# The shared expert's down product split into three short-format products, in an attention and mixture-of-experts block

## The chip, the cores and the metric

The kernel runs on one core of a Trainium2 chip, as one program. The metric is its device time in microseconds, the median of several executions. A profile is taken from one more execution.

## The reference

x has 8 batches of 256 tokens with 256 features. First a modulated layer norm and attention with 16 query and 8 key heads; its result goes through a gate and is added to x. Then the part that matters here: a second modulated norm, an RMS norm, and two things added up: 32 routed experts (each token goes to four of them, with at most 128 tokens per expert), and one shared expert that every token passes:

```python
sh = jax.nn.silu(x @ sw_gate) * (x @ sw_up) @ sw_down   # 256 -> 704 -> 256
sh = jax.nn.sigmoid(x @ w_shared_gate) * sh
out = out + sh
return inp + out.reshape(Bq, Sq, Hq)
```

All arrays are float32.

## The kernel before

The 2048 tokens are handled as four pairs of batches, q = 0 to 3, 512 tokens each. The text calls them quarters. The order of work of each engine is written out by hand, one function per engine, and semaphores join the engines. Each engine runs its instructions in the written order.

**Attention** takes the first 566 us: 128 steps, with the work after attention for pair q spread over the steps of pair q+1 (`hooks`). The last pair has no such cover, and its work (`post_gate`, `post_stats`, `post_h2`, `post_squares`, `post_rms`, `post_xn`, `post_xnt`, then logits, choice of experts, slots) is mixed by hand with the shared expert of pair 0.

**The shared expert** of a quarter has two parts. `gate_up(q, f)` makes inner rows in six pieces, f = 0 to 5: five of 128 rows and one of 64 (704 = 5 x 128 + 64). Each piece is made with 12 products of 512 columns (6 in the last piece, where gate and up share one), in the short format: sums of hi x hi, hi x lo and lo x hi, where hi is the value rounded to the format float32r and lo is what is left (`halves`, lines 1287 to 1293). ScalarE then takes the silu of the gate (`silu_of`, into one of two halves of `sg2`), and VectorE multiplies it by the up part (`hidden`, into `hs`). `down(q, t)` (lines 1482 to 1494) makes the 128 output rows of token tile t, t = 0 to 3, by six float32 products, one for each piece, of 128 tokens by 256 features. The result is scaled and put into `shrow`.

**Order after attention.** Gate/up of quarter 0 (two pieces already between the last attention steps), down of quarter 0 around the last pair's router (`post_logits`, `post_prefix`), gate/up and down of quarter 1, the 32 experts (`expert_slot`), then gate/up and down of quarters 2 and 3. While quarters 2 and 3 run, GpSimd and VectorE combine the experts' sums (`combine`): GpSimd for quarters 1 and 2, VectorE for quarters 0 and 3, VectorE's steps for quarter 3 lying between its `hidden(LAST, ...)`.

**Queues.** Loads go out from SP in a fixed order. The experts' weights and rows sit in a ring of eight, and a load for expert e waits until expert e - 8 has been used. The first rows of experts are loaded when all scatters are done (`st_scat`); GpSimd issues these, and some of them wait for a tile or a piece of quarter 1 (`PRODUCT`, `TILE`, lines 816 to 823).

**Memory.** Buffers are laid out like a stack; what is allocated after `att.close()` lies where attention's buffers were.

Of the kernel before, what the change touches and what calls it, by code (L numbers as in the profile page):

```python
# [5 lines left out]
F32 = mybir.dt.float32  # L6
# [44 lines left out]
def adaln_block(nc, x, w_pack, w_o, conv_k, conv_v, w_norm, w_router, w_gate, w_up, w_down, sw_gate, sw_up,  # L51
                sw_down, w_sgate, c_in, wmod, cos_t, sin_t, mask_t, ident_t, tri_t, ebase_t, out):
    ctx = ExitStack()
    with ctx:
# [127 lines left out]
        hs = sb("hs", [PN, FT, TOK])  # L182
        sg2 = sb("sg2", [PN, 2, TOK])
        swd = sb("swd", [PN, FT, H])
        shrow = sb("shrow", [PN, NPAIR * TT, H])
# [8 lines left out]
        gball = sb("gball", [PN, B, H])  # L194
        fin = sb("fin", [PN, NPAIR, TT, H])
        first_sums = sb("first_sums", [PN, NSUM, TT, H])
# [25 lines left out]
        def gu_banks(q, f):  # L222
# [43 lines left out]
            sem(n) for n in ("sw_hi_done", "sw_lo_done", "sh_ps", "sg2_done", "hs_done", "dn_ps", "shrow_done"))  # L266

# [203 lines left out]
        def _(act):  # L471
# [184 lines left out]
            def silu_of(q, f):  # L656
                act.wait_ge(sh_ps, FT * q + (f + 1))
                if f >= 2 or later(q):
                    act.wait_ge(hs_done, FT * q + (f - 1))
                gate, up = gu_banks(q, f)  # L660
                if f < FT - 1:
                    act.activation(sg2[:, f % 2, :], gate[:, :], ACT.Silu).then_inc(sg2_done, 1)
                else:
                    act.activation(sg2[0:FR, f % 2, :], up[FR:2 * FR, :], ACT.Silu).then_inc(sg2_done, 1)

            def shared_rows(q, t):
                act.wait_ge(dn_ps, TT * q + (t + 1))
                act.activation(shrow[:, TT * q + t, :], DN[t % 2][:, 0:H], ACT.Copy, scale=sgate[:, q, t:t + 1]).then_inc(shrow_done, 1)
# [15 lines left out]
            silu_of(0, 1)  # L684
            silu_of(0, 2)
            act.preload_act_table_set("natural_log_exp_and_others")
            post_std(LAST, 0, 2)
            silu_of(0, 3)
            post_squares(LAST, 0)
# [3 lines left out]
            silu_of(0, 4)  # L693
            silu_of(0, 5)
            post_xnt(LAST, 0)
# [5 lines left out]
            for f in range(FT):  # L701
                silu_of(1, f)
# [4 lines left out]
            for q in range(2, NPAIR):  # L707
                for f in range(FT):
                    silu_of(q, f)
# [6 lines left out]
        def _(pool):  # L716
# [123 lines left out]
            def with_shared(q):  # L840

                rows_q = shrow[:, TT * q:TT * (q + 1), :]
# [14 lines left out]
            def combine(q):  # L857
                a = sums(q, 0)
                pool.wait_ge(ld_sums[q], 16 * NSUM)
                for i in range(1, NSUM):  # L860
                    own(pool.tensor_tensor(a, a, sums(q, i), ALU.add))
                own(pool.tensor_tensor(batches(a), batches(a), gate_of(q), ALU.mult))
                f = fin[:, q, :, :]
                if q == 1:
                    pool.tensor_tensor(f, f, a, ALU.add).then_inc(fin_done[q], 1)
                else:
                    pool.wait_ge(ld_bas[q], 16)
                    own(pool.tensor_tensor(f, f, a, ALU.add))
                    pool.wait_ge(shrow_done, TT * (q + 1))
                    pool.tensor_tensor(f, f, shrow[:, TT * q:TT * (q + 1), :], ALU.add).then_inc(fin_done[q], 1)  # L870
# [6 lines left out]
        def _(dve):  # L877
# [293 lines left out]
            def hidden(q, f):  # L1171
# [30 lines left out]
            for f in range(FT):  # L1202
                hidden(1, f)
# [53 lines left out]
            def shared_rows(q, t):  # L1257
                dve.wait_ge(dn_ps, TT * q + (t + 1))
                dve.scalar_tensor_tensor(shrow[:, TT * q + t, :], DN[t % 2][:, 0:H], sgate[:, q, t:t + 1],
# [5 lines left out]
            for f in range(FT):  # L1265
                hidden(2, f)
# [7 lines left out]
            hidden(LAST, 1)  # L1274
            combine(LAST, 3)
            for f in range(2, FT):
                hidden(LAST, f)
            for t in range(TT):
                shared_rows(LAST, t)
                dve.wait_ge(shrow_done, TT * LAST + (t + 1))  # L1280
                dve.tensor_tensor(fin[:, LAST, t, :], fin[:, LAST, t, :], shrow[:, TT * LAST + t, :],
# [4 lines left out]
        def _(pe):  # L1286
# [289 lines left out]
            pe.wait_ge(ld_swd, 32)  # L1576
# [67 lines left out]
```

## Time and profile before

| | us |
|---|---|
| median of 3 runs | 781.05 (780.67 to 781.09) |
| the profiled execution, device time | 779.91 |
| its span, first to last instruction | 778.1 |
| TensorE busy | 744.3 (96% of the span) |
| weight loads busy | 617.3 (79%) |
| VectorE, ScalarE, GpSimd busy | 536.7, 441.9, 425.7 |
| granted TensorE clock, mean | 0.998 |

In the profile PE is TensorE's products, PEld its weight loads, DVE VectorE, ACT ScalarE, POOL GpSimd, and SP the engine whose queue carries most of the DMAs. A row of the chain of waits says from when, for how long and by whom the path to the end was held. A busy TensorE is not TensorE at its peak: records of products overlap, so their pace is read from starts and from pieces of the chain, not from the length of a single record. An f32 product appears as two records, a short-format product as one.

### The profile page before, as it was taken

To read this page: it belongs to the slowest core of one execution; us is meant where nothing else is said; L and a number is where in the kernel's file an instruction comes from. 1 tells how busy PE (TensorE), PEld (TensorE's weight loads), DVE (VectorE), ACT (ScalarE), POOL (GpSimd) and SP (SyncE) were. 2 spreads that over 40 slices of the span, in tenths; PEclk is the share of its full clock that TensorE was granted. 3 is DMA by queue.
4 is the path that set the end of the run, shared out by engine and by line. 5 is a ranking of instruction groups with operands and counts; after the bars stand their busy time and mean duration, and the time that the engine had idled before them with its cause. 6 is when DMAs were issued, how large, how long until landed. Compare 5 with 4: busy or idle time off the path is not lost.

```text
span 778.1 us, 12285 instructions
## 1 busy us (share of the span) xinstructions
PE 744.3 (96%) x3858; PEld 617.3 (79%) x3858; DVE 536.7 (69%) x1676; ACT 441.9 (57%) x1145; POOL 425.7 (55%) x337
## 2 busy tenths in 40 slices
PE   3899999999999999999999999999989999989998
PEld 3688778888888888788888888888876777756765
DVE  4698777679877777987786798778664234534283
ACT  4687766766876576677657667766553222212110
POOL 0644445554556378646637865654544527656366
PEclk9999999999999999999999999999999999999999
DMA  8950006700005011100401101050358669997762
GB/s 301 313 130 1 2 1 207 249 1 1 1 1 174 17 39 47 39 0 1 141 23 39 46 28 45 31 161 2 122 148 265 147 189 288 271 253 149 183 203 81
DMA packets 62351, 84.45 MB, mean 109 GB/s; under 512 B 6312, under 2 KB 50229, under 8 KB 62288
## 3 DMA queue, kind: packets, MB, share of 16 engines
q1 hardware_dynamic: 52880, 73.52, 31.1%
q0 software_dynamic: 7680, 8.95, 5.8%
q10 hardware_dynamic: 1728, 1.21, 0.6%
q8 instruction: 31, 0.51, 0.3%
q14 instruction: 32, 0.26, 0.1%
HBM read 54.88 MB, written 33.51 MB: 114 GB/s over the span
## 4 chain that ended last, share of the span: by engine, by line
PE 78%; DVE 10%; DMA 5%; ACT 3%; issue 2%; SPq 1%; POOL 1%; ACTq 0%; POOLq 0%
PE PJ L1292 23%; PE OUT L1396 12%; PE U L1385 6%; PE U L1345 6%; PE U L1374 5%; DMA xe<-slot_rows 4%; PE U L1546 3%; PE U L1344 3%; PE U L1386 3%; PE OUT L1492 3%; PE U L1492 3%; PE U L1292 2%; PE XB L1292 2%; PE XB L1368 1%; DVE U L945 1%
## 5 line engine op out<-in xcount | busy, mean ns | idle before, releaser
L736 POOL TENSOR_TENSOR qsw<-qsw,sinT 128x512 f32<-128x512 f32 x96 | 124.2, 1294 | 214.8 <-ACT qsw L523 214.1
L536 ACT ACTIVATE U<-U,nmax 128x128 f32<-128x128 f32 (+1 forms) x256 | 98.9, 386 | 79.2 <-DVE nmax L945 79.0
L945 DVE CUSTOM_DVE_ANT_0 U<-U,mask 128x128 f32<-128x128 f32 (+1 forms) x256 | 86.6, 379 | 74.9 <-PE U L1345 74.7
L1396 PE MATMUL OUT<-wo,oT 128*128 128x256 f32 x512 | 131.5, 380 | 0.0
L1292 PE MATMUL PJ<-hT_hi,w_hi 128*128 128x512 f32 x256 | 113.5, 443 | 4.3 <-DVE hT_lo L919 3.9
L1292 PE MATMUL PJ<-hT_lo,w_hi 128*128 128x512 f32 x256 | 102.2, 399 | 0.0
L1292 PE MATMUL PJ<-hT_hi,w_lo 128*128 128x512 f32 x256 | 102.2, 399 | 0.0
L955 DVE TENSOR_SCALAR prob<-U,rinv 128x128 f32<-128x128 f32 (+1 forms) x256 | 95.1, 413 | 4.5
L522 ACT ACTIVATE qsw<-PJ 64x512 f32<-64x512 f32 x96 | 57.0, 593 | 67.1 <-PE PJ L1292 61.7
L740 POOL TENSOR_TENSOR qr<-qr,qsw 128x512 f32<-128x512 f32 x64 | 82.9, 1295 | 18.5 <-DVE qr L933 14.8
L1396 PEld LDWEIGHTS OUT<-wo,oT 128*128 128x128 f32 x512 | 87.6, 191 | 6.6
L747 POOL DMA_INDIRECT slot_rows<-xn,sidx x64 | 64.4, 1006 | 44.2 <-issue 11.1
L1385 PE MATMUL U<-pT,vN 128*128 128x256 f32 x256 | 77.0, 382 | 1.9 <-ACT pT L544 1.8
L1345 PE MATMUL U<-kc,qr 128*128 128x256 f32 x256 | 76.8, 382 | 0.0
L830 POOL DMA_INDIRECT expert_sum<-ye,slot_token x32 | 49.7, 1552 | 42.3 <-DMA expert_sum<-ye,slot_token 22.4
L544 ACT ACTIVATE pT<-U 128x384 f32<-128x384 f32 x128 | 62.4, 488 | 9.4 <-PE U L1374 5.7
L1374 PE MATMUL U<-ident,prob 128*128 128x128 f32 x384 | 62.9, 273 | 0.4 <-DVE prob L955 0.4
L1344 PEld LDWEIGHTS U<-kc,qr 128*128 128x128 f32 x256 | 47.7, 190 | 19.1 <-issue 4.6
L1374 PEld LDWEIGHTS U<-ident,prob 128*128 128x128 f32 x384 | 49.9, 141 | 13.5 <-DVE prob L955 0.8
L1292 PEld LDWEIGHTS PJ<-hT_hi,w_hi 128*128 128x128 f32 x256 | 49.1, 192 | 13.0 <-DVE hT_lo L919 4.3
L1292 PEld LDWEIGHTS PJ<-hT_hi,w_lo 128*128 128x128 f32 x256 | 49.1, 192 | 11.7
L960 DVE COPY oT<-U 128x256 f32<-128x256 f32 x128 | 54.0, 422 | 4.9 <-PE U L1386 4.9
(201 smaller groups left out, 1557.3 us busy)
## 6 DMA issues: line engine op xcount, KB each, us to landing
wgu<-in_dram SPq DMA_DIRECT2D x32, 352.0 KB
expert_sum<-blank SPq DMA_DIRECT2D x3, 2176.0 KB, 17.7
wd<-in_dram SPq DMA_DIRECT2D x16, 352.0 KB
slot_rows<-blank SPq DMA_DIRECT2D x1, 4624.0 KB, 26.8
xe<-slot_rows SPq DMA_DIRECT2D x16, 289.0 KB
late_sums<-expert_sum SPq DMA_DIRECT2D x9, 512.0 KB, 9.8
wraw<-in_dram SPq DMA_DIRECT2D x8, 512.0 KB, 12.1
bcm<-mod_rows SPq DMA_DIRECT2D x8, 512.0 KB, 6.7
```

What stands on the lines that cost most here:

```text
L536: last = act.activation(U[n % 3][:, a:z], U[n % 3][:, a:z], ACT.Exp, scale=-1.0, bias=nmax[:, n % 4, j:j + 1], accum_out=rsum[:, n % 4, j: ...
L736: pool.tensor_tensor(pair3(qsw[:, n % NQSW, :]), pair3(qsw[:, n % NQSW, :]), both(sinT[:, :]), ALU.mult).then_inc(t2_done, 1)
L740: pool.tensor_tensor(rope_buffer(m), rope_buffer(m), qsw[:, n % NQSW, :], ALU.add).then_inc(rope_done, 1)
L747: pool.indirect_dma_start(out=slots_d, out_offset=bass.IndirectOffsetOnAxis(ap=sidx[:, c:c + 1], axis=0), in_=xn[:, p % 2, c // TOPK, :], ...
L945: last = dve.tensor_tensor_reduce(out=U[n % 3][:, a:z], in0=U[n % 3][:, a:z], in1=mask[:, a:z], scale=-float(HD) ** -0.5, scalar=3.4e38, o ...
L955: last = dve.tensor_scalar(prob[:, n % 2, a:z], U[n % 3][:, a:z], rinv[:, n % 4, j:j + 1], None, ALU.mult)
L1292: last = pe.matmul(out_ap, a(c), b_(c), start=(n == 0), stop=(n == len(steps) - 1))
L1344: pe.matmul(U[n % 3][:, 0:PN], q[:, 0:PN], k[:, 0:PN], start=True, stop=True)
L1345: pe.matmul(U[n % 3][:, PN:3 * PN], q[:, PN:S], k, start=True, stop=True).then_inc(sc_ps, 1)
L1374: last = pe.transpose(U[n % 3][:, j * PN:(j + 1) * PN], prob[:, n % 2, j * PN:(j + 1) * PN], ident[:, :])
L1385: pe.matmul(o, v[:, 0:PN], pT[:, n % 2, 0:S], start=True, stop=False)
L1396: last = pe.matmul(OUT[b][:, t * H:(t + 1) * H], oT[:, n % NOT, t * PN:(t + 1) * PN], wo[:, head, :], start=(head == 0 and t == 0), stop=( ...
```

## The change

The down product gets the same form as gate/up. Both of its operands are split. ScalarE makes the high parts by a copy into float32r (`hidden_high` for a piece of the inner rows, `down_high` once for the weights), and VectorE makes the low parts by subtraction (`hidden_low`, `down_low`). `hidden` now writes its product in place into `sg2`, and so a half of `sg2` is free for the next silu only when `hidden_low` has read it: `silu_of` waits for `hs_lo_done` of the piece two before. `down` waits for `hs_lo_done` where it waited for `hs_done`, and has 18 products in place of six. `gate_up` still waits for `hs_done`. `shrow` keeps two quarters instead of four, `sums` of quarter 0 lie over the experts' buffers, and `gball` and `fin` move down.

```diff
-        hs = sb("hs", [PN, FT, TOK])
+        hs_hi = sb("hs_hi", [PN, FT, TOK], F32R)
+        hs_lo = sb("hs_lo", [PN, FT, TOK], F32R)
         sg2 = sb("sg2", [PN, 2, TOK])
-        swd = sb("swd", [PN, FT, H])
-        shrow = sb("shrow", [PN, NPAIR * TT, H])
+        raw_d = ExitStack()
+        swd = sb("swd", [PN, FT, H], F32, raw_d)
+        raw_d.close()
+        shrow = sb("shrow", [PN, 2 * TT, H])
+        swd_hi = sb("swd_hi", [PN, FT, H], F32R)
+        swd_lo = sb("swd_lo", [PN, FT, H], F32R)
+        gball = sb("gball", [PN, B, H])
+        fin = sb("fin", [PN, NPAIR, TT, H])
+
+        sums_at = ExitStack()
+        first_sums = sb("first_sums", [PN, NSUM, TT, H], F32, sums_at)
+        sums_at.close()
...
@@ ScalarE
                 if f >= 2 or later(q):
-                    act.wait_ge(hs_done, FT * q + (f - 1))
+                    act.wait_ge(hs_lo_done, FT * q + (f - 1))
...
+            def hidden_high(q, f):
+                fw = min(PN, FS - f * PN)
+                act.wait_ge(hs_done, FT * q + (f + 1))
+                if f == 0 and later(q):
+                    act.wait_ge(dn_ps, TT * q)
+                act.activation(hs_hi[0:fw, f, :], sg2[0:fw, f % 2, :], ACT.Copy).then_inc(hs_hi_done, 1)
+
+            def down_high():
+                act.wait_ge(ld_swd, 32)
+                act.activation(swd_hi[:, 0:FT - 1, :], swd[:, 0:FT - 1, :], ACT.Copy)
+                act.activation(swd_hi[0:FR, FT - 1, :], swd[0:FR, FT - 1, :], ACT.Copy).then_inc(swd_hi_done, 1)
...
             silu_of(0, 0)
             silu_of(0, 1)
+            hidden_high(0, 0)
             silu_of(0, 2)
+            hidden_high(0, 1)
             act.preload_act_table_set("natural_log_exp_and_others")
             post_std(LAST, 0, 2)
             silu_of(0, 3)
+            hidden_high(0, 2)
+            down_high()
             post_squares(LAST, 0)
             post_squares(LAST, 1)
             act.preload_act_table_set("natural_log_exp_and_others")
             post_rms(LAST)
             silu_of(0, 4)
+            hidden_high(0, 3)
             silu_of(0, 5)
+            hidden_high(0, 4)
+            hidden_high(0, 5)
             post_xnt(LAST, 0)
             post_xnt(LAST, 1)
             shared_rows(0, 0)
...
-            for f in range(FT):
-                silu_of(1, f)
+            for f in range(FT + 1):
+                if f < FT:
+                    silu_of(1, f)
+                if f > 0:
+                    hidden_high(1, f - 1)
...
@@ VectorE
                 dve.wait_ge(sg2_done, FT * q + (f + 1))
-                if f == 0 and later(q):
-                    dve.wait_ge(dn_ps, TT * q)
-                dve.tensor_tensor(hs[0:fw, f, :], gu_banks(q, f)[1][0:fw, :], sg2[0:fw, f % 2, :], ALU.mult).then_inc(hs_done, 1)
+                g = sg2[0:fw, f % 2, :]
+                dve.tensor_tensor(g, gu_banks(q, f)[1][0:fw, :], g, ALU.mult).then_inc(hs_done, 1)
+
+            def hidden_low(q, f):
+                fw = min(PN, FS - f * PN)
+                dve.wait_ge(hs_hi_done, FT * q + (f + 1))
+                dve.tensor_tensor(hs_lo[0:fw, f, :], sg2[0:fw, f % 2, :], hs_hi[0:fw, f, :].bitcast(F32),
+                                  ALU.subtract).then_inc(hs_lo_done, 1)
+
+            def down_low():
+                dve.wait_ge(swd_hi_done, 1)
+                dve.tensor_tensor(swd_lo[:, 0:FT - 1, :], swd[:, 0:FT - 1, :], swd_hi[:, 0:FT - 1, :].bitcast(F32), ALU.subtract)
+                dve.tensor_tensor(swd_lo[0:FR, FT - 1, :], swd[0:FR, FT - 1, :], swd_hi[0:FR, FT - 1, :].bitcast(F32),
+                                  ALU.subtract).then_inc(swd_lo_done, 1)
...
             post_stats(LAST, 0)
             post_stats(LAST, 1)
+            hidden_low(0, 0)
             hidden(0, 2)
+            hidden_low(0, 1)
             post_h2(LAST, 0)
             post_h2(LAST, 1)
             hidden(0, 3)
+            hidden_low(0, 2)
+            down_low()
             post_xn(LAST, 0)
             post_xn(LAST, 1)
             hidden(0, 4)
+            hidden_low(0, 3)
             hidden(0, 5)
+            hidden_low(0, 4)
+            hidden_low(0, 5)
             post_xnt(LAST, 0)
             post_xnt(LAST, 1)
...
             hidden(LAST, 0)
             combine(LAST, 2)
             hidden(LAST, 1)
+            hidden_low(LAST, 0)
             combine(LAST, 3)
-            for f in range(2, FT):
-                hidden(LAST, f)
+            for f in range(2, FT + 1):
+                if f < FT:
+                    hidden(LAST, f)
+                hidden_low(LAST, f - 1)
...
@@ TensorE
                 if t == 0:
-                    pe.wait_ge(hs_done, FT * (q + 1) - 1)
+                    pe.wait_ge(hs_lo_done, FT * (q + 1) - 1)
...
                     if t == 0 and f == FT - 1:
-                        pe.wait_ge(hs_done, FT * (q + 1))
-                    last = pe.matmul(DN[t % 2][:, 0:H], hs[0:fw, f, t * PN:(t + 1) * PN], swd[0:fw, f, :],
-                                     start=(f == 0), stop=(f == FT - 1))
+                        pe.wait_ge(hs_lo_done, FT * (q + 1))
+                    for i, (h, w) in enumerate(((hs_hi, swd_hi), (hs_hi, swd_lo), (hs_lo, swd_hi))):
+                        last = pe.matmul(DN[t % 2][:, 0:H], h[0:fw, f, t * PN:(t + 1) * PN], w[0:fw, f, :],
+                                         start=(f == 0 and i == 0), stop=(f == FT - 1 and i == 2))
...
-            pe.wait_ge(ld_swd, 32)
+            pe.wait_ge(swd_lo_done, 1)
             down(0, 0)
```

The loops for quarters 1 to 3 are changed alike on both engines. VectorE also waits for `based` >= 2 before `shared_rows(2, 0)`.

## Rows read from the trace of the kernel before

**Rows 1.** The page, chain that ended last, shares of the span by engine.

```profile
PE 78%; DVE 10%; DMA 5%; ACT 3%; issue 2%; SPq 1%; POOL 1%; ACTq 0%; POOLq 0%
```

**Rows 2.** Chain of waits in order of time, 574 to 593 us: start, duration, what.

```profile
574.94 0.60 ACT sg L662
...
577.38 0.89 DVE h L999 x2
...
583.21 0.21 ACT rms L572
...
586.43 3.02 PE OUT L1492 x12
589.45 2.80 PE XB L1292 x24
```

**Rows 3.** The same chain in quarters 1, 2 and 3.

```profile
616.07 1.40 PE U L1292 x6
617.48 3.05 PE OUT L1492 x12
...
729.71 2.79 PE PJ L1292 x12
...
751.03 0.69 DVE hs L1177
...
762.90 3.05 PE OUT L1492 x12
```

**Rows 4.** Weight loads in order of time, first tiles of quarter 2.

```profile
733.93 2.02 PEld L1492 LDWEIGHTS OUT<-swd,hs 128*128 128x128 f32 x10 [0.47 <-issue]
736.28 0.29 PEld L1492 LDWEIGHTS OUT<-swd,hs 64*128 64x128 f32 x2 [0.33 <-issue]
736.91 2.02 PEld L1492 LDWEIGHTS U<-swd,hs 128*128 128x128 f32 x10 [0.33 <-issue]
```

**Rows 5.** Two of the logits' products in order of time, eleven apart.

```profile
590.74 0.26 PE L1292 MATMUL XB<-wr_hi,xnT_hi 128*128 128x34 f32 x1
...
591.97 0.26 PE L1292 MATMUL XB<-wr_hi,xnT_lo 128*128 128x34 f32 x1
```

**Rows 6.** Lines 505, 919 and 556: duration in ns, least/median/most.

```profile
L505 ACT ACTIVATE hT_hi<-hst x8: 619/623/630, 15.2 to 363.3; 128x512 fp32r<-128x512 f32 x8
L919 DVE TENSOR_TENSOR hT_lo<-hst,hT_hi x8: 680/692/1127, 15.8 to 381.5; 128x512 fp32r<-128x512 f32 x8
L556 ACT ACTIVATE w_hi<-wraw x8: 1040/1054/1057, 9.9 to 83.2; 128x1024 fp32r<-128x1024 f32 x8
```

**Rows 7.** VectorE and GpSimd in order of time; then line 765 by shape.

```profile
743.45 1.22 DVE L1244 TENSOR_TENSOR first_sums<-first_sums,gball 128x1024 f32<-128x1024 f32 x1
...
751.64 2.69 DVE L1244 TENSOR_TENSOR late_sums<-late_sums,gball 128x1024 f32<-128x1024 f32 x1
...
746.60 6.65 POOL L861 TENSOR_TENSOR late_sums<-late_sums 128x1024 f32<-128x1024 f32 x2 [19.69 <-DMA late_sums<-expert_sum]
753.33 3.25 POOL L862 TENSOR_TENSOR late_sums<-late_sums,gball 128x1024 f32<-128x1024 f32 x1
...
764.79 2.34 POOL L862 TENSOR_TENSOR late_sums<-late_sums,gball 128x1024 f32<-128x1024 f32 x1
...
769.71 2.42 POOL L870 TENSOR_TENSOR fin<-fin,shrow 128x1024 f32<-128x1024 f32 x1
...
L765 POOL TENSOR_TENSOR h<-h,bcm 128x512 f32<-128x512 f32 x8 | 10.2, 1274 | 0.0
```

**Rows 8.** Stretches: busy time by engine, granted clock, DMA share, GB/s.

```profile
617.50:629.50 12.00, 12.00 (x49) 8.48 (x49) 0.68 (x1) 2.01 (x4) 5.18 (x6) 1.00 0.19 53
629.50:673.00 43.50, 43.22 (x207) 33.33 (x208) 21.16 (x72) 10.92 (x36) 21.83 (x13) 1.00 1.00 270
```

**Rows 9.** SP's issues in order of time, first rows of experts.

```profile
626.41 1.76 SPq L432 DMA_DIRECT2D xe<-slot_rows  x4
```

**Rows 10.** Products at the start of attention, in order of time.

```profile
18.16 0.80 PE L1292 MATMUL PJ<-hT_hi,w_hi 128*128 128x512 f32 x1 [3.90 <-DVE hT_lo L919]
...
23.44 0.65 PE L1292 MATMUL PJ<-hT_hi,w_hi 128*128 128x512 f32 x1
```

More of the change, by code:

```diff
@@ L193, in adaln_block @@
         slot_token = sb("slot_token", [PN, E], I32)
-        gball = sb("gball", [PN, B, H])
-        fin = sb("fin", [PN, NPAIR, TT, H])
-        first_sums = sb("first_sums", [PN, NSUM, TT, H])
         def sums(q, i):
@@ L266, in adaln_block @@
             sem(n) for n in ("sw_hi_done", "sw_lo_done", "sh_ps", "sg2_done", "hs_done", "dn_ps", "shrow_done"))
+        hs_hi_done, hs_lo_done, swd_hi_done, swd_lo_done = (
+            sem(n) for n in ("hs_hi_done", "hs_lo_done", "swd_hi_done", "swd_lo_done"))
         class Chain:
@@ L664, in silu_of @@
                     act.activation(sg2[0:FR, f % 2, :], up[FR:2 * FR, :], ACT.Silu).then_inc(sg2_done, 1)
+            def hidden_high(q, f):
[8 more added lines that the diff above has]
+                act.activation(swd_hi[0:FR, FT - 1, :], swd[0:FR, FT - 1, :], ACT.Copy).then_inc(swd_hi_done, 1)
             def shared_rows(q, t):
                 act.wait_ge(dn_ps, TT * q + (t + 1))
-                act.activation(shrow[:, TT * q + t, :], DN[t % 2][:, 0:H], ACT.Copy, scale=sgate[:, q, t:t + 1]).then_inc(shrow_done, 1)
+                act.activation(shrow[:, TT * (q % 2) + t, :], DN[t % 2][:, 0:H], ACT.Copy, scale=sgate[:, q, t:t + 1]).then_inc(shrow_done, 1)
             def expert_slot(n):
@@ L707, in _ @@
             for q in range(2, NPAIR):
-                for f in range(FT):
-                    silu_of(q, f)
+                for f in range(FT + 1):
+                    if f < FT:
+                        silu_of(q, f)
+                    if f > 0:
+                        hidden_high(q, f - 1)
             for t in range(TT):
@@ L840, in with_shared @@
             def with_shared(q):
-                rows_q = shrow[:, TT * q:TT * (q + 1), :]
+                rows_q = shrow[:, TT * (q % 2):TT * (q % 2 + 1), :]
                 pool.wait_ge(shrow_done, TT * (q + 1))
@@ L869, in combine @@
                     pool.wait_ge(shrow_done, TT * (q + 1))
-                    pool.tensor_tensor(f, f, shrow[:, TT * q:TT * (q + 1), :], ALU.add).then_inc(fin_done[q], 1)
+                    pool.tensor_tensor(f, f, shrow[:, TT * (q % 2):TT * (q % 2 + 1), :], ALU.add).then_inc(fin_done[q], 1)
             combine(1)
@@ L1201, in _ @@
             post_keys(LAST)
-            for f in range(FT):
-                hidden(1, f)
+            for f in range(FT + 1):
+                if f < FT:
+                    hidden(1, f)
+                if f > 0:
+                    hidden_low(1, f - 1)
             def expert_slot(n):
@@ L1258, in shared_rows @@
                 dve.wait_ge(dn_ps, TT * q + (t + 1))
-                dve.scalar_tensor_tensor(shrow[:, TT * q + t, :], DN[t % 2][:, 0:H], sgate[:, q, t:t + 1],
+                dve.scalar_tensor_tensor(shrow[:, TT * (q % 2) + t, :], DN[t % 2][:, 0:H], sgate[:, q, t:t + 1],
                                          gball[:, 2 * q + t // 2, :], ALU.mult, ALU.mult).then_inc(shrow_done, 1)
@@ L1264, in _ @@
             dve.wait_ge(ld_gb, 16)
-            for f in range(FT):
-                hidden(2, f)
+            for f in range(FT + 1):
+                if f < FT:
+                    hidden(2, f)
+                if f > 0:
+                    hidden_low(2, f - 1)
+            dve.wait_ge(based, 2)
             for t in range(TT):
@@ L1274, in _ @@
             hidden(LAST, 1)
+            hidden_low(LAST, 0)
             combine(LAST, 3)
-            for f in range(2, FT):
-                hidden(LAST, f)
+            for f in range(2, FT + 1):
+                if f < FT:
+                    hidden(LAST, f)
+                hidden_low(LAST, f - 1)
             for t in range(TT):
@@ L1280, in _ @@
                 dve.wait_ge(shrow_done, TT * LAST + (t + 1))
-                dve.tensor_tensor(fin[:, LAST, t, :], fin[:, LAST, t, :], shrow[:, TT * LAST + t, :],
+                dve.tensor_tensor(fin[:, LAST, t, :], fin[:, LAST, t, :], shrow[:, TT * (LAST % 2) + t, :],
                                   ALU.add).then_inc(fin_done[LAST], 1)
```

## The prediction, made before the changed kernel was run

> **What bounds the kernel now.** The chain of waits comes first. TensorE holds 78% of it, VectorE 10% [rows 1], so what a change does to TensorE's own stream is paid in full, unless TensorE waits for somebody. Then the parts of the chain that hold the down product. In the handover of the last pair (574.9 to 592.3 us) the chain leaves TensorE and runs over ScalarE and VectorE: a silu, `post_h2`, the root mean square, and only then the first down tile and the router's logits [rows 2]. In the second shared stage (quarter 1, the second pair of batches) the last gate/up piece is followed by the down tile with no gap, and so in quarter 2 [rows 3, 4]. In the last quarter the chain goes to VectorE again: `hidden(3,0)` at 751.03 comes late because VectorE is combining expert sums [rows 3]. The stretches show what the experts' stage is limited by: the DMA engines are 0.19 busy before it and 1.00 from its first microsecond [rows 8]. Its loads are released by the experts' progress, so a later start of it moves its end by as much; nothing there absorbs a delay.
>
> **The tile itself.** A down tile is six f32 products, which the profile shows as twelve records, 2.98 us from 733.93 to 736.91 [rows 4]. Ten of them are loaded in 2.02, a pace of 0.215 us; around the two of 64 rows the weight loads sit idle for 0.33 us on each side, as they wait until the products ahead have left the array. The new tile is 18 short-format products, 15 on 128 rows and 3 on 64. Such a product of 512 columns takes 2.79 us / 12 = 0.232 [rows 3], which is 0.213 of streaming (512 columns at 2.4 GHz, the level of the granted clock here) and some 0.019 besides. Products of 34 columns, where only the weight load can bind, follow each other every (591.97 - 590.74) / 11 = 0.112 [rows 5]. For 256 columns the ends are 0.112 and 0.107 + 0.019 = 0.126; I take 0.125: streaming (0.107) and the fixed part seen at 512 columns add up to more than the weight load. The two stalls stay. Today 2.98 less ten steps of 0.215 leaves 0.83 for them; a short product streams 0.107 less before each, which leaves about 0.60, and with 14 + 2 steps of 0.125 the tile is 2.60. That is 0.38 less per tile (0.60 less at the low end). Of 16 tiles, 15 are on the chain; the second one lies under the routing's VectorE work. Gain 15 x 0.38 = 5.7 us, the low end 9.0.
>
> TensorE: Matmul & The Clock Gate in the Trainium skill (Back-to-back issue gap) gives 262 cycles for 256 free columns, an estimate of 0.109 us each; the tile would be 0.60 + 16 x 0.109 = 2.35 and the time some 4 us below my sum. No row here has this shape.
>
> **The splits.** Per piece of the hidden rows: a ScalarE copy of 128x512, 0.62 us, and a VectorE subtract, 0.69 (0.68 to 1.13) [rows 6]. In the middle of a quarter a gate/up piece lasts 2.79 on TensorE and silu plus product take 0.60 + 0.69 [rows 2, 3], so another 1.31 hides. At the end of a quarter it does not. Counted from the end of gate/up (T), the piece before the last is finished at T-1.40 [rows 3]. Its silu and product end at T-0.05. The new order: `hidden_high(3)` ends at T-0.15, `hidden_low(3)` at T+0.6, and since `silu_of(5)` now waits for that (same `sg2` half), silu(5) ends at T+1.2, `hidden_high(4)` behind it at T+1.8, `hidden(5)` at T+1.9, `hidden_low(4)` at T+2.5. `down(q,0)` waits for that one: +2.5 us in quarters 1 and 2 against a start at once today. Bounds: +1.9 (if only the one order ScalarE high then VectorE low counted) and +3.0 (a slow subtract). The sixth piece's low part arrives inside the first tile and costs nothing.
>
> **Quarter 0.** Here each added instruction stands ahead of the chain of rows 2. `silu_of(0,2)` waits for `hidden_low(0,0)`, queued on VectorE behind the statistics (done 576.2), so it runs at 576.95 instead of 574.94; with `hidden_high(0,1)` ahead of the table change, `post_h2` starts at 579.9 instead of 577.4: +2.5. On ScalarE then `hidden_high(0,2)` (0.6) and `down_high` (1.05 for 1024 columns [rows 6], so 1.27 for 1280 and 0.4 for the tail) push the squares; `post_rms` starts at 587.0 instead of 583.2: +3.8. `down_low` on VectorE (1.5 + 0.5, ends 586.8) is hidden by this. Behind `post_xn` come silu(4), low(3), silu(5), high(4), low(4) in turn, and GpSimd's four `post_base` operations of 1.27 [rows 7] compete with the subtracts. Down starts at about 593.0 instead of 586.4, the logits wait for `post_xnt` behind `hidden_low(0,5)` and end at 599.0 against 592.25 [rows 2]: +7.0 net, first tile's saving in it (so +7.4 for the splits). Bounds: +4 (VectorE never held up, table and squares as today) and +9.
>
> **First experts.** The load of the first rows is issued at 626.41 [rows 9], 2.9 after the second tile of quarter 1; it was there when TensorE came at 629.5. The two tiles after that are 0.76 shorter together, and up to all of it can turn into a wait for that load: I take 0.4 (0 to 0.8).
>
> **The last quarter.** GpSimd adds expert sums from 746.60 to 772.1 and VectorE combines at the same time. Look at the durations: VectorE's 1024-column operation is 1.22 alone and 2.69 beside GpSimd; GpSimd's is 2.34 alone and 3.25 beside VectorE [rows 7]. The operation of 751.64 ends 1.1 after GpSimd's second one (746.60 + 6.65 = 753.25) and GpSimd's next, 753.33, ends 2.34 after that. So they take turns, each waiting for the whole of the other; the f32 product from PSUM (0.69 at 751.03) is not held up. Each `hidden_low(3,f)` has two SBUF operands like the combine, so it waits for the rest of a 2.34 operation, and the next silu waits for it. Run through in order, with the experts' shift left out: down(2) starts 2.5 late and ends 1.0 late, which puts `combine(0,3)` beside GpSimd; hidden(3,0) at 754.3 (was 751.0); low(0) ends 760.8, hidden(3,2) 765.0, low(1) 767.35, hidden(3,3) 768.8, low(2) 770.3, low(3) 773.3, silu(5) 773.9, low(4) 776.3. `down(3,0)` starts at 776.35, and did at 762.90 [rows 3]: 13.5 late, of which 1.0 came from quarter 2, so +12.5.
>
> SBUF — State Buffer in the Trainium skill (SBUF: two separate sides) says that the pair of ports that VectorE and GpSimd share is an exclusive lock for the whole instruction, and no split of bandwidth; by it the sum stays as it is. The durations alone would also fit a plain stretch by 2.2. Then a subtract is 1.5 at most (1.13 is the longest shown [rows 6]), `down(3,0)` starts near 771.3, and this term is +7.5. The lock fits the end times of rows 7, the stretch does not, so I take +12.5 and keep +7.5 as the other bound.
>
> **Edits at nothing.** The new places of the buffers (their loads are already behind the waits that free them), `shrow` with two halves, and the wait for `based` (its work is done at expert 12, 60 us before). If a cover failed, the cost would be one wait of the GpSimd operation behind it, up to 3 us.
>
> **Sum.** Quarter 0 +7.0; six tiles in quarters 0 and 1 -2.3; handover 1 +2.5; load +0.4; handover 2 +2.5; four tiles -1.5; last quarter +12.5; four tiles -1.5. Together +19.6. The profiled execution is 779.91 us (778.1 of span and 1.8 around), 1.1 below the median; I add the sum to the median 781.05: 800.6.
>
> **The clock.** TensorE would idle about 3.7 us twice and 6 us once. The trace shows such an idle only at the start: after 3.90 us idle the 512-column products run every (23.44 - 18.16) / 12 = 0.44 us, the 1.2 GHz level, for 5 us [rows 10]. If it falls before `down(3,0)`, 5.3 us of tiles at half pace lose 2.6. I take 0, since no fall from the full level is shown; the upper bound is 2 x 2.6.
>
> **Rivals.**
> *Stretch, not lock.* VectorE's subtracts are slowed in proportion. Last quarter +7.5, quarter 0 about +6: 794.6. For it: the median of rows 6 is 0.69 although GpSimd is busy in much of that stage. Against: the end times.
> *Short products bound by the weight load.* 2.38 per tile: 15 x 0.22 = 3.3 less, about 797.3.
> *Clock falls once or twice.* 803.2 to 805.8.
> *The cover holds, faster.* The splits of the last pieces disappear under other work, as those in mid-quarter do, and only the tiles count: 781.05 - 5.7 = 775.4. It decides from the point where all waits of the handovers together stay under 5.7 us. For it: ScalarE and VectorE idle over 2 us per piece in the quarters. Against: only 1.40 us of gate/up lies behind the piece waited for, and quarter 0 is ScalarE's and VectorE's own chain.
> *The change does not do what it says.* If the short format took two passes at 256 columns, a product is 0.215, the tile 0.60 + 16 x 0.215 = 4.0, 15 x 1.0 = 15 and the lost 5.7 more: 821. The 512-column row speaks against it.
>
> **Chances.** Forecast 0.47, stretch 0.18, short products 0.12, clock 0.13, two passes 0.03, the cover holding 0.03, partly holding so that gain and loss cancel 0.04 (half of it each way out of the band). Range 789 to 807: from the stretch with short products and a cheaper quarter 0 up to two clock falls. A change under 0.2% (1.6 us) can't be told from none. Faster 0.04, same 0.03, slower 0.93.
>
> **What would show it.** In the profile after: a tile of 18 products in about 2.60 us with two idle stretches of the weight load left; idle of 2.5 us ahead of `down(1,0)` and `down(2,0)`, released by a subtract; the logits about 7 later; subtracts over 1.5 us beside GpSimd in the last quarter, and silus that wait for them; the experts' stage as long as before. It is wrong if the first tile of a quarter starts within 1 us, if subtracts beside GpSimd stay at 0.69, or if the experts' stage gets shorter by what came before.

## The result, and the profile after

The changed kernel took 801.41 us (798.89 to 803.93, four executions), beside 781.07 us (780.67 to 783.43, four) for the kernel before: a ratio of 1.0242, interval [1.0205, 1.0279]. Medians are taken over all executions of a kernel, while a ratio leaves out those that the slower state of a chip lengthened, among them the profiled one of experiment 5 and two of the four of experiment 2, and so is not the quotient of the medians. The forecast was 800.6. Its profiled execution has a span of 797.1 us against 778.1, so 19.0 longer.

From the page of the changed kernel, the granted clock in 40 slices of the span and the chain's shares by engine:

```profile
PEclk9999999999999999999999999999979789999997
...
PE 79%; DVE 11%; ACT 5%; issue 3%; DMA 1%; POOL 1%; SPq 0%; ACTq 0%; DVEq 0%; POOLq 0%
```

Most engine shares of the chain look like those of before [rows 1]: VectorE 11% for 10, ScalarE 5% for 3. But DMA fell from 5% to 1%, some 30 us, which is a first sign of what happened in the experts' stage. The clock row has dips near 600, 620 to 640 and 780 us; before it stood at 9 throughout. Neither row says where 19 us went, stage by stage. The chain in order of time does. This is it at the end of gate/up in quarter 0, where before only a silu, `post_h2`, `rms` and the tile stood [rows 2]:

```profile
576.61 0.60 ACT sg L672
...
581.97 1.16 ACT swd_hi L685
...
586.48 0.21 ACT rms L582
...
589.56 2.00 DVE hs_lo L1216
...
592.94 1.51 DVE hs_lo L1216
594.59 3.82 PE OUT L1556 x18
...
601.41 3.75 PE U L1556 x18
```

And in quarters 1, 2 and 3 (compare [rows 3], where the tile follows gate/up at once):

```profile
628.18 0.61 DVE hs_lo L1216
...
628.84 4.51 PE OUT L1556 x18
633.34 4.43 PE U L1556 x18
637.78 4.30 PE OUT L1556 x18
642.08 2.53 PE U L1556 x18
...
743.28 2.67 issue
745.95 2.58 PE OUT L1556 x18
...
778.61 1.36 DVE hs_lo L1216
...
780.02 4.51 PE OUT L1556 x18
784.52 4.31 PE U L1556 x18
...
791.36 2.55 PE U L1556 x18
```

Two things are to be seen. The low part of an inner row now stands ahead of the first tile of each quarter. And the same 18 products take 2.53 us in one tile and 4.3 to 4.5 in another (3.8 in two of quarter 0).

The stretches say what the second one is (columns as in [rows 8]; the granted clock is the figure before the DMA share):

```profile
620.00:630.00 10.00, 7.37 (x32) 5.87 (x31) 5.74 (x9) 4.37 (x8) 6.33 (x6) 0.91 0.02 0
630.00:640.00 10.00, 10.00 (x43) 9.10 (x42) 0.00 (x0) 0.95 (x2) 2.91 (x3) 0.50 0.02 2
740.00:750.00 10.00, 7.33 (x46) 6.14 (x45) 5.66 (x9) 3.11 (x6) 0.00 (x0) 1.00 0.84 262
```

The granted clock is 0.50 in the second stretch, that is 1.2 GHz, after 2.63 us in which TensorE had nothing. In the third, in quarter 2, it stays at 1.00 after an idle of 2.67 us.

Stage by stage, from the end of one stage to the end of the next on TensorE, in the two profiled executions:

| stretch | predicted | measured |
|---|---|---|
| to the end of the router's logits (592.25 -> 601.41) | +7.0 | +9.2 |
| other tiles of quarter 0, gate/up of quarter 1 | -0.8 | -0.4 |
| handover and tiles of quarter 1 | +1.0 | +6.4 |
| 32 experts (88.7 -> 83.0 us) | +0.4 | -5.7 |
| quarter 2 | +1.0 | +0.8 |
| last quarter, up to `down(3,0)` (17.0 -> 23.9) | +12.5 | +6.9 |
| last four tiles | -1.5 | +1.9 |
| sum | +19.6 | +19.0 (rounded rows: 19.1) |

So the sum is right and four of its lines are off by 3 to 6 us: the tiles of quarter 1, the experts, the last quarter, the last four tiles. Three things lie behind them: the clock, the experts' stage, and what VectorE and GpSimd do to each other in the last quarter. The experiments are about these three.

### The profile page after: what moved, and what is told of

Same layout as the page of the kernel before. It is cut to its first block, busy times and chain, and to the rows that moved or that the text cites. A ratio compares the mean times of both kernels' runs of the same rounds, so it can differ in the third digit from the quotient of the medians.

```text
span 797.1 us, 12532 instructions
## 1 busy us (share of the span) xinstructions
PE 749.1 (94%) x3954; PEld 632.2 (79%) x3954; DVE 563.1 (71%) x1702; ACT 456.3 (57%) x1171; POOL 427.8 (54%) x337
## 4 chain that ended last, share of the span: by engine, by line
PE 79%; DVE 11%; ACT 5%; issue 3%; DMA 1%; POOL 1%; SPq 0%; ACTq 0%; DVEq 0%; POOLq 0%
PE PJ L1355 22%; PE OUT L1459 12%; PE U L1448 6%; PE U L1408 6%; PE U L1610 5%; PE U L1437 4%; PE OUT L1556 3%; PE U L1556 3%; PE U L1407 3%; PE U L1449 3%; PE U L1355 2%; DVE hs_lo L1216 2%; PE OUT L1629 2%; PE XB L1629 2%; PE XB L1355 2%
## 5 line engine op out<-in xcount | busy, mean ns | idle before, releaser
L775 POOL TENSOR_TENSOR qr<-qr,qsw 128x512 f32<-128x512 f32 x64 | 82.8, 1294 | 18.7 <-DVE qr L968 15.0
## 6 DMA issues: line engine op xcount, KB each, us to landing
wraw<-in_dram SPq DMA_DIRECT2D x8, 512.0 KB, 11.5
```

Source lines behind the costliest of these rows:

```text
L775: pool.tensor_tensor(rope_buffer(m), rope_buffer(m), qsw[:, n % NQSW, :], ALU.add).then_inc(rope_done, 1)
```

## The experiments

A ratio is always against the kernel before on the same chip; where no interval is given there were not enough executions for one.

**1. The products alone** (layout and order of before, no splits).

```diff
-        hs = sb("hs", [PN, FT, TOK])
+        hs = sb("hs", [PN, FT, TOK], F32R)
...
-                    last = pe.matmul(DN[t % 2][:, 0:H], hs[0:fw, f, t * PN:(t + 1) * PN], swd[0:fw, f, :], ...
+                    for i in range(3):
+                        last = pe.matmul(DN[t % 2][:, 0:H], hs[0:fw, f, t * PN:(t + 1) * PN],
+                                         sw_hi[0:fw, f // 3, (f % 3) * H:(f % 3 + 1) * H], ...
```

> The kernel before with 18 short-format products per down tile and no splits: hidden writes float32r, every piece is multiplied three times, and the moving operand is a slice of the gate/up weights, so the low parts and the down weights are left out. If the tile is worth what the trace after shows at the full clock (2.53 against 2.98 us) and nothing else matters: 15 x 0.45 = 6.7 us less, 774.3. Rival, the experts' stage gives back what comes earlier (it took back 5.7 us of a delay in the trace after): the eight tiles of quarters 0 and 1 are lost, 781.1 - 3.6 = 777.5.

Measured: 779.7 us (772.27 to 783.46), ratio 0.9978 [0.9937, 1.0018]; the span is 774.7, 3.4 below that of before. Its chain of waits, quarters 0 and 1:

```profile
591.59 3.90 PE U L1493 x18
...
596.13 2.33 PE OUT L1493 x18
...
622.48 2.10 DMA slot_rows<-xn,sidx
...
624.60 2.81 DMA xe<-slot_rows
```

A full-speed tile is 2.53. With 15 tiles at 0.45 less that would be 6.7. One tile ran at a lowered clock (3.90), and at the experts TensorE waited 0.7 us for their first rows, which were what ended last there. The term "0.4 (0 to 0.8)" of the prediction is this wait. The changed kernel doesn't meet it in its profiled execution, and for 0.8 us in each of two repeats.

Even so the last tile ends 7.4 us earlier than before (767.5 for 774.9). More than half of that is lost behind it, and not on TensorE. This is GpSimd's last addition here; in the kernel before it is at 769.71 [rows 7]:

```profile
766.70 2.41 POOL L870 TENSOR_TENSOR fin<-fin,shrow 128x1024 f32<-128x1024 f32 x1
```

It ends 1.6 us after the last tile, where before it ended 2.8 ahead of it. In both traces a closing drain of GpSimd, which the views don't count as work, takes 7.76 us from the start of that addition. It ends at 777.4 of 778.1 before, and at 774.4 of 774.7 here, where every other engine had been done since 772.8. So the kernel before has under 1 us to give at its end unless GpSimd starts earlier too, and GpSimd starts when the experts' sums are loaded (746.6 before, 745.3 here).

**2. The splits alone** (all else as in the changed kernel, tiles of six float32 products).

```diff
-                    for i, (h, w) in enumerate(((hs_hi, swd_hi), (hs_hi, swd_lo), (hs_lo, swd_hi))):
-                        last = pe.matmul(DN[t % 2][:, 0:H], h[0:fw, f, t * PN:(t + 1) * PN], w[0:fw, f, :], ...
+                    last = pe.matmul(DN[t % 2][:, 0:H], hs_hi[0:fw, f, t * PN:(t + 1) * PN].bitcast(F32),
+                                     swd_hi[0:fw, f, :].bitcast(F32), ...
```

> The changed kernel with all its splits and waits, but six float32 products per tile, of the high parts alone (the low parts are made and not used). Theory one, TensorE's clock falls because it idles ahead of the down tiles: the falls stay, each tile costs 0.45 more at the full clock and about 1 at half, so 801.4 + 15 x 0.45 and up to 3 more: 808 to 811. Theory two, the clock falls because of the short products' own pattern: no falls, about 9 us of slow tiles gone, 799.

Measured: 811.12 us (801.42 to 814.3) beside 781.61: three of four executions at 808 or above, as the first theory has it, one at 801. Chain of waits, `down(0,0)`, then quarters 1 and 2:

```profile
593.30 5.75 PE OUT L1555 x12
599.05 5.23 PE XB L1355 x24
...
634.39 3.05 PE OUT L1555 x12
...
745.49 2.67 issue
748.16 4.45 PE OUT L1555 x12
```

The float32 tiles run at half clock too (5.75 for 3.02). So it doesn't take the new products to lower the clock. But here quarter 1, after the same idle, keeps its clock and quarter 2 loses it: the reverse of the changed kernel. An idle of 2.7 us is not followed by a fall each time.

**3. TensorE kept busy in the handovers.** Products into a bank that is overwritten afterwards, 10, 11, 11 and 21 of 512 columns for the four quarters.

```diff
+FILL = (10, 11, 11, 21)
...
+                if t == 0:
+                    for _ in range(FILL[q]):
+                        pe.matmul(DN[0][:, :], sw_hi[:, 0, 0:PN], sw_hi[:, 0, 512:1024], start=True, stop=True)
+                    pe.wait_ge(hs_lo_done, FT * (q + 1) - 1)
```

> The changed kernel, with 10, 11, 11 and 21 extra 512-column products on unused data ahead of the wait of down(q,0), which end within the idle time (2.6 us in quarters 1 and 2, 5.2 in 3). If idle time is what lowers the clock, the tiles of quarters 1 and 3 go back from 4.5 to 2.53: 5.6 and 3.8 us less on TensorE, of which the experts' stage may take back what it absorbed: 792 to 796. If the clock falls for another reason: 801.

Measured: 798.42 us (797.78 to 800.29), ratio 1.0219 [1.0148, 1.0291], so against the changed kernel's 1.0242 no difference that these intervals show. A stretch of quarter 1, then the chain of the last tiles:

```profile
630.00:640.00 10.00, 9.87 (x72) 8.70 (x70) 1.00 (x2) 1.81 (x4) 4.09 (x4) 1.00 0.07 10
```

```profile
780.57 4.78 PE OUT L1552 x21
785.35 2.34 PE OUT L1559 x18
...
792.75 2.55 PE U L1559 x18
```

The clock stays up in quarter 1 and in the last tiles, so in these two places the idle time was what brought it down (the mean granted clock is 0.984 to 0.989 in the four executions, 0.974 to 0.978 in all those of the changed kernel); in quarter 0 it falls even so (the tiles behind the logits take 3.75 and 3.98). Handover and tiles of quarter 1 take 12.8 us for the changed kernel's 18.4, and the last four tiles 9.9 for 13.9. These 9.5 us don't arrive in the total. The experts' stage is 88.1 in this execution, not 83.0, and the last quarter up to `down(3,0)` is 28.1, not 23.9. Both are taken up below.

**4. The kernel before, with its experts' stage started 15 us late** (65 products ahead of the experts, nothing else).

```diff
+            for _ in range(DELAY):
+                pe.matmul(PJ[0][:, :], sw_hi[:, 0, 0:PN], sw_hi[:, 0, 512:1024], start=True, stop=True)
```

> The kernel before with 65 extra 512-column products (65 x 0.232 = 15.1 us) between down(1,3) and the experts, so that the experts start as late as they did in the changed kernel; nothing else differs. The prediction's step (nothing in the experts' stage absorbs a delay): 781.1 + 15.1 = 796.2. Rival, the stage absorbs 5.7 us of it, as the trace after suggests, because its DMAs find free engines or the first eight experts' loads and the accumulations are out of the way: 790.4.

Measured: 798.43 us (795.0 to 801.84), ratio 1.0207 [1.0132, 1.0282]. The experts' stage starts 20 us later than before (15.0 of them the products, 4.9 nearly all from a fall of the clock in quarter 0):

```profile
634.41 14.97 PE PJ L1589 x65
...
738.85 2.79 PE PJ L1293 x12
```

It ran from 649.4 to 738.5 (the first record of gate/up begins 0.35 ahead of its step in the chain), 89.1 us against 88.7. In the kernel before, a late start of the stage is handed on in full; this part of the prediction holds.

**5. The subtracts of the last quarter with one operand in PSUM.**

```diff
-                dve.tensor_tensor(hs_lo[0:fw, f, :], sg2[0:fw, f % 2, :], hs_hi[0:fw, f, :].bitcast(F32),
+                g = XB[0:fw, :] if q == LAST else sg2[0:fw, f % 2, :]
+                dve.tensor_tensor(hs_lo[0:fw, f, :], g, hs_hi[0:fw, f, :].bitcast(F32),
```

> The changed kernel; in the last quarter the subtract reads its first operand from PSUM (a bank that is free by then, so the low parts of that quarter are not the right values), with the same length, place and waits. Lock theory (a VectorE operation with two SBUF operands waits for the whole GpSimd operation, one with a PSUM operand doesn't): the five subtracts of 2.17, 2.15, 1.46, 1.44 and 1.36 us in the trace after go back to 0.69, down(3,0) starts 4 to 5 us earlier, and if the idle time ahead of it gets too short for the clock to fall, up to 3.8 more: 793 to 797. Stretch theory (VectorE is slowed beside GpSimd whatever it reads): 801.

Measured: 803.77 us (797.6 to 811.87), ratio 1.0245 [1.0159, 1.0331]. VectorE in the last quarter, first of the changed kernel:

```profile
763.35 2.17 DVE L1216 TENSOR_TENSOR hs_lo<-sg,hs_hi 128x512 fp32r<-128x512 f32 x1
...
772.98 1.46 DVE L1216 TENSOR_TENSOR hs_lo<-sg,hs_hi 128x512 fp32r<-128x512 f32 x1
```

and then of this experiment, with GpSimd operations that it runs beside:

```profile
780.00 0.68 DVE L1217 TENSOR_TENSOR hs_lo<-XB,hs_hi 128x512 fp32r<-128x512 f32 x1
780.59 2.11 DVE L1308 TENSOR_TENSOR fin<-fin,late_sums 128x1024 f32<-128x1024 f32 x1
...
774.94 6.67 POOL L896 TENSOR_TENSOR late_sums<-late_sums 128x1024 f32<-128x1024 f32 x2
781.69 3.27 POOL L897 TENSOR_TENSOR late_sums<-late_sums,gball 128x1024 f32<-128x1024 f32 x1
```

All subtracts take 0.68 while GpSimd works on as before, and the idle time ahead of `down(3,0)` is 2.6 us, not 5.2. With both operands in SBUF the same instruction takes anything from 0.68 to 2.17 by where in a GpSimd operation it falls, and in these rows never more than the rest of one. The subtract of 763.35, for one, ends 0.55 us after GpSimd's pair of operations that began at 758.59 and ended at 764.97 (shown further down). That is taking turns; the stretch rival is out. SBUF — State Buffer in the Trainium skill (SBUF: two separate sides) states just this: the shared pair is an exclusive lock, taken by a VectorE operation with two SBUF inputs against one of GpSimd that reads SBUF. The trace agrees, 2.17 against 0.68. The gain is where it was expected: from `hidden(3,0)` to `down(3,0)` it is 14.9 us, for 20.2 in the changed kernel. But the total does not show it, and the 793 to 797 us expected were missed. In this profile GpSimd began its additions 2.2 us before the last tile of quarter 2 ended (2.5 after it in the changed kernel), VectorE's combining stood in line behind them, and `hidden(3,0)` came 11.3 us after that tile, not 3.7; so the last quarter up to `down(3,0)` took 26.2 us, not 23.9. The last four tiles took 15.8 us at a fallen clock, and up to the end of quarter 2 it ran behind the changed kernel by 8.7.

**6. Quarter 0 left in float32**, quarters 1 to 3 as changed (`down_high` and `down_low` moved behind the router's logits).

```diff
+SHORT = [(1, 0), (1, 1), ..., (3, 5)]
...
+                    if not is_short(q, f):
+                        last = pe.matmul(DN[t % 2][:, 0:H], hs[0:fw, f, t * PN:(t + 1) * PN], swd[0:fw, f, :], ...
```

> The changed kernel with quarter 0 as before (float32 products on an unsplit buffer), and the weights split after the last pair's softmax numerators, under quarter 1. My theory: quarter 0's splits are 9.2 us late at the end of the logits (601.41 against 592.25), and all of it comes back, less about 1.1 for the two dearer tiles on the chain: 801.4 - 8.1 = 793.3. Rival, the weights' split in its new place delays the routing or quarter 1 by as much as it did: 798 to 801.

Measured: 797.05 us (789.83 to 798.59), ratio 1.0155 [1.0067, 1.0242]. The logits end at 594.0 instead of 601.4, so 7.4 us of quarter 0 are the splits' and their clock's. In the profiled execution only 0.7 of them are left at the end: the last quarter takes 27.7 us up to `down(3,0)` and not 23.9, the experts 85.8 and not 83.0, and the clock falls in quarter 2 as well but for less in quarter 1. By the ratios, 1.0155 against 1.0242, more is left, but their intervals overlap.

**7. Short format only in quarters 1 and 2**, six pieces each, with three buffers in `sg2` instead of two, and with TensorE waiting for one piece at a time in the first tile. The weights are split where experiment 6 splits them.

```diff
+SHORT = [(1, 0), (1, 1), ..., (1, 5), (2, 0), (2, 1), ..., (2, 5)]
+DEPTH = 3
```

> Short format in quarters 1 and 2 alone, with three buffers for the silu (so that silu(5) no longer waits for the subtract of piece 3) and TensorE waiting piece by piece in the first tile. Quarters 0 and 3 as before. Each of the two quarters saves 4 x 0.45 = 1.8 and waits 0.7 in its first tile: 781.4 - 2.2 = 779.2. Rival, the handover is set by the subtracts whatever TensorE does with the early pieces (2.5 us late): 781.4 + 1.4 = 782.8.

**8. Only pieces 0 to 3 of those two quarters**; pieces 4 and 5, whose splits have no cover, stay in float32.

```diff
+SHORT = [(1, 0), (1, 1), (1, 2), (1, 3), (2, 0), (2, 1), (2, 2), (2, 3)]
```

> As the one before, but the last two pieces of quarters 1 and 2 stay in float32, so that nothing is split behind the end of gate/up. A tile is 2.53 + 0.14 = 2.67 to 2.75, no wait at the handover: 8 x 0.27 = 2.2 less, 779.2. If the mixture of formats costs a stall at each change (as the change to 64 rows does, 0.2 each): 781.

Measured: 775.63 us (770.51 to 780.54), ratio 0.9922 [0.9882, 0.9963] for the seventh, and 776.81 us (773.22 to 779.12), 0.9921 [0.9888, 0.9955] for the eighth. The kernel before had 784.65 us there (775.23 to 788.89). So both are faster by 0.8%, which is little beside that scatter but clear of it. Chain of waits of the eighth in quarter 2:

```profile
730.52 1.39 PE U L1385 x6
731.91 1.43 PE OUT L1594 x12
733.34 1.06 PE OUT L1590 x4
734.40 1.63 PE U L1594 x12
```

The tile starts with no gap, as before the change, and takes 2.69 where it took 2.98. Four of them are 10.7 for 12.0 us in both quarters. That is 2.5 us; the ratio stands for some 6. (In the seventh the splits of pieces 4 and 5 are still waited for inside the first tile, and quarter 2 has 12.4 us of tiles, because the last one waits for expert sums that VectorE combines ahead of it.) The experts' stage is shorter again: 85.4 us here and 82.8 in the seventh, where it was 88.7.

Not all of this reaches the end. In both profiles the span ends with GpSimd's drain, as in experiment 1: its last addition ends at 765.4 and 770.1, the span is 771.0 and 775.6. So the faster tiles of quarter 2 took nothing off these executions' ends. They are shorter than the one before by 7.1 and 2.5 us because GpSimd started 5.1 and 0.5 earlier, its additions took 24.0 us and not 25.5, and the rest was slack.

**9 to 12. The two kernels again, twice each, on one chip.**

> The changed kernel itself, once more, to see how much one execution's experts' stage differs from another's. If the 5.7 us by which that stage was shorter in the changed kernel's profiled execution (83.05 against 88.75) belong to the execution, the stage is anywhere between 82 and 89.5 us here; if the late start of the stage itself shortens it (what the sum had at nothing), it is 83 to 84 again. The clock falls for down(0,0), down(1,0) and down(3,0) again if the idle time ahead of them is what lowers it, each time over the first three tiles.

> The kernel before itself, once more. By scatter its experts' stage differs from 88.75 us by some microseconds in either direction; if the stage absorbs what comes late in the changed kernel alone, it is 88 to 89.5 again.

> As for the first repeat of the changed kernel: an experts' stage of 83 to 84 us if a late start shortens it, anywhere from 82 to 89.5 if it is the execution's.

> As for the first repeat of the kernel before: an experts' stage of 88 to 89.5 us if the length belongs to the kernel, anywhere from 82 to 89.5 if it is the execution's.

Measured: 797.58 and 797.52 us changed, 782.91 and 786.84 before, beside a third one of before of 781.01. The experts' stage, from the last tile of quarter 1 to the first gate/up product of quarter 2:

| | us |
|---|---|
| before, three profiled executions | 88.7, 92.0, 88.3 |
| layout of before: experiments 1 and 4 | 87.5, 89.1 |
| changed, three profiled executions | 83.0, 83.7, 84.1 |
| new layouts (that of the changed kernel: 2, 3, 5; two more of their own: 6, and 7 and 8) | 83.4, 88.1, 88.0, 85.8, 82.8, 85.4 |

So it is not the one execution. The stage is 4 to 9 us shorter in the changed kernel, every time. A late start is not the reason (experiment 4; and the seventh starts it earliest and has it shortest). The DMA queues of that stage, first before and then changed (packets, MB, share of the 16 engines' time):

```profile
q1 hardware_dynamic: 11066, 18.14, 68.7%
q0 software_dynamic: 3744, 3.41, 26.7%
```

```profile
q1 hardware_dynamic: 10954, 17.91, 67.3%
q0 software_dynamic: 3600, 3.28, 27.6%
```

A packet of the experts' loads costs 0.687 x 16 x 88.7 / 11066 = 88 ns of an engine's time before and 82 after; packets of the scatters cost the same in both (101 and 102). The DMA engines are 0.96 and 0.95 busy. That the shorter stage comes from the cheaper packets is an argument from this, not an experiment. Its other side is on the chain. In the kernel before it leaves TensorE in this stage for

```profile
681.14 27.87 DMA xe<-slot_rows x2
```

and TensorE waits six times, 4.3 us together, for rows of experts. In the changed kernel it waits for no rows there, the chain stays on TensorE but for some 6 us, and TensorE's idle time in the stage is 2.3 us and not 6.6.

It is not every packet that is cheaper. Of the two commonest sizes, 1408 and 2048 bytes, the median packet takes 60 and 98 ns in both kernels; the means are 73.5 and 110 before, 67.5 and 104 after. So the difference lies in the slower packets. The cheaper mean goes with the new places of the buffers in most kernels, yet experiments 3 and 5 have the places of the changed kernel and 86 and 87 ns. What makes them slower stays open: no run here changed the places alone.

The same repeats explain the last quarter. GpSimd's first operation there waits for a load of expert sums. This is it in the changed kernel and in experiment 6:

```profile
758.59 6.38 POOL L896 TENSOR_TENSOR late_sums<-late_sums 128x1024 f32<-128x1024 f32 x2 [19.83 <-DMA late_sums<-expert_sum]
```

```profile
751.49 6.29 POOL L919 TENSOR_TENSOR late_sums<-late_sums 128x1024 f32<-128x1024 f32 x2 [19.98 <-DMA late_sums<-expert_sum]
```

In the changed kernel that is 2.5 us after the last tile of quarter 2 (756.1; 2.5 and 2.8 in the repeats), and the last quarter takes 23.9 in all three executions. In experiment 6 it is 0.2 us ahead of that tile's end (751.7), and the quarter takes 27.7; in experiment 3 0.7 ahead, and 28.1; in experiment 2 5.1 ahead, and 28.1. Against 17.0 before that is +6.9 where GpSimd comes late and +10.8 and +11.1 where it comes in time to stand in VectorE's way. The lateness hangs together with the experts' stage: from that stage's start to GpSimd's first addition it is 117.1 us before and 114.0 in the changed kernel, so the sums came 3.1 earlier, and TensorE's last tile of quarter 2, counted from the same start, 5.0 earlier.

## Why the prediction was right, and where its parts were not

The mechanism was right: the splits of the last pieces have no cover, they cost more than the products give, and most of the cost is in quarter 0 and in the last quarter. Point by point:

- **The tile**: 2.60 predicted, 2.53 measured at full clock. A product of 256 columns follows the last every 0.120 us, between the bounds; the two stalls around the 64-row products stay. The weight-load rival (2.38) is out, and so are the 0.109 us that the prediction gave beside its own figure. The two-pass rival is out.
- **The handovers**: +2.5 predicted, 2.63 and 2.67 measured.
- **Quarter 0**: +7.0 predicted, +9.2 measured. The order of instructions ran as worked out: the third silu at 576.61 (I had 576.95), `post_rms` at 586.48 (587.0). The logits end at 601.4 where I had 599.0: the first tile starts 1.6 later (594.6 for 593.0, subtracts beside GpSimd that took up to 2.07), runs 1.2 longer at a lowered clock, the logits 0.2 longer, and the 0.6 of wait for `post_xnt` that I had counted ahead of them isn't there.
- **The load of the experts' rows**: 0.4 predicted, 0 to 0.8 in three executions, inside the bounds.
- **The last quarter**: +12.5 predicted, +6.9 measured. The step that failed is the one that laid GpSimd's operations beside VectorE's "with the experts' shift left out". It moved both together. In fact GpSimd's start hangs on the load of the sums, and it came 2.5 us after the last tile of quarter 2, where it had come 0.7 after; so `combine(0,3)` and the next operation ran alone (1.22 each), and `hidden(3,0)` was at 759.86, 3.7 after the last tile, where the prediction had it 7.4 after. Taken in that order the lock fits, and where GpSimd does come in time the term is 10.8 to 11.1. (One reading under it was off by little: GpSimd's operation of 753.33 ends 2.25 us after VectorE's, not 2.34.)
- **The clock**: taken as 0, with an upper bound of 2 x 2.6. This is the term that was furthest off. Seven tiles of the profiled execution ran slow: 3.82 + 3.75 + 4.51 + 4.43 + 4.30 + 4.51 + 4.31 = 29.6 for 7 x 2.53 = 17.7, so 11.9 us. Of these some 0.7 did not count, because the second tile of quarter 0 lies beside the routing on VectorE; 11.2 are left. I had let a fall last as long as the one after the start and let it come once or twice; it came in three quarters of four. And I had put the term at nothing "since no fall from the full level is shown". That was a misreading: the trace of before shows one, without any idle time, right behind 24 products of 34 columns. The page, in slices of 19 us, rounds it to a 9:

```profile
252.70:256.10 3.40, 3.40 (x10) 2.71 (x10) 0.77 (x3) 0.83 (x2) 0.00 (x0) 0.50 0.33 115
```

- **The experts' stage**: "as long as before" was wrong, it was 5.7 shorter. That nothing there absorbs a delay was right. The prediction named as a sign of failure a stage that gets shorter by what came before. The stage did get shorter, but as far as experiment 4 and the seventh show not by its late start; the cause is open.
- **What is paid in full**: the prediction began with this, for all that a change does to TensorE's stream. It fails for time taken off. Experiment 1 lost 4.0 of 7.4 us to GpSimd's drain, so the 775.4 of the rival in which the cover holds could hardly have been reached by the tiles alone.

So 19.6 less 5.6 for the last quarter, less 6.1 for the experts, plus 11.2 for the clock is 19.1, and small terms of either sign (tiles 0.07 faster each, quarter 0 apart from its clock 0.9 dearer) leave 19.0. That the direction and the places of the cost came out was the mechanism; that the number came within 1 us was luck, because the clock's error cancelled the other two, which hang together. The range from 789 to 807 held it, but its upper side had room for a fall of the clock of 5.2, not 11.2.

## What to carry to other kernels

Before a faster form is given to an operation, look at what has to be ready for its first instance in each stage: here the short form gave something only in the two quarters without a contended VectorE, 0.8%, as much with the two uncovered pieces as without them, and the traces don't tie most of that to the products. Look also at which engine ends the program: time taken off TensorE came through only as far as GpSimd's own end allowed. A gap of 2.5 us put ahead of TensorE costs its length and may cost more than that again in clock (5.6 us in quarter 1). Filling the gap gave the second part back, and it was lost again further on, in stages held by DMA and by GpSimd. A sum that comes out right is no proof of its terms: compare them stage by stage, over more than one execution.

## What the hardware showed that was not expected

- Behind an idle of 2.63 us TensorE's granted clock was 0.50 for 13 us; after one of 2.67 it stayed at 1.00, in the same execution. Two repeats of the same kernel lost it in the same three quarters, for 11.5 and 11.7 us of tiles in quarter 1 instead of 15.8. The kernel before can lose it as well, and without a long idle. In one of its repeats, with no idle over 1.5 us ahead, it fell within the logits, 24 products of 34 columns, and the tile behind them took 5.60 us (in experiments 1, 4, 6 and 8 it fell within the logits or right behind them):

```profile
589.62 3.25 PE XB L1292 x24
592.87 5.60 PE U L1492 x12
```

- A VectorE subtract of 512 columns takes 0.68 us with one operand in PSUM and up to 2.17 with both in SBUF, beside the same GpSimd operations.
- The same loads of the experts' stage took 82 to 83 ns per packet in one kernel and 88 to 89 in the other, three executions each, with the same median packet.
- GpSimd's closing drain took 7.7 to 8.1 us from the start of its last addition in every execution profiled, and ended the program in experiments 1, 7 and 8.
